# First loads beside the constants, time steps in eight matmuls, B by C in another bank, and running sums spread for half of the heads and both tiles at a time

## The chip, the cores and the metric

One core of one Trainium2 chip runs the whole program. The metric is the device time of one execution in microseconds; lower is better. Shown are the median of three runs and one profiled execution.

## The reference

Three layers act on 4096 tokens of 512 values, with a residual connection each: a feed-forward layer with a half weight, a Mamba-2 layer, and the same feed-forward layer again. Cut to what matters here:

```
# feed-forward: layer norm, 64 experts of which each token takes 4, and two shared experts
out = sum over the token's 4 experts of weight * down(silu(gate(h)) * up(h)) + shared(h)
x = x + 0.5 * out
# Mamba-2, batch 2, 2048 tokens, 8 heads of 128, state 128
proj = rmsnorm(layernorm(x)) @ in_proj_w            # gate 1024, ssm 1024, dt 8, B 128, C 128
ssm = silu(causal_conv4(ssm)); dt = softplus(dt + dt_bias)
cum = cumsum(A * dt)                                # the running sums, per head
y = (exp(cum_i - cum_j) * (C_i . B_j), j <= i) @ (dt * x)  +  exp(cum_i) * C_i @ state
state = exp(cum_end) * state + B' @ (exp(cum_end - cum_j) * dt * x)
x = x + ((y + D * ssm) * silu(gate)) @ out_proj_w
```

## The kernel before

Three phases follow each other on every engine, without a barrier between them: `ffn` "a" (to about 740 us), `mamba` (740 to 1645 us) and `ffn` "b". Matmuls whose inputs need full precision are split in high and low parts (`three`, lines 1568 to 1571: high by high, high by low, low by high), in `fp32r`. Each engine has its own program, written out by hand; the engines meet only in semaphores, so that a step starts when its engine has done all that stands ahead of it and its waits are met. Names: PE is TensorE, DVE VectorE, ACT ScalarE, POOL GpSimd, SP the engine that issues loads and stores.

**Mamba.** 16 blocks of 256 tokens (two tiles of 128). A projection writes 256 columns into one of two halves of the bank pair `p_ab`; the jobs of a block form a ring, and `ab(n, job)` waits until ACT has copied out the job two places before (`ab_free`). Gates 2 and 3 go to `p_x` instead. On PE a block is (`block_`, from line 1705): ssm 0 and 1, `cumulate` (running sums), the second half of the block before's output projection, ssm 2, `b_by_c`, `spread(0)`, ssm 3 to 5, `spread(1)`, ssm 6 and 7, gates 0 to 7, `x_to_tokens(0)`, `turn` (turns the next block's rows), `x_to_tokens(1)`, `y_product(0)`, `state_product(0)`, `head` (projections of dt, C and B for the next block), `y_product(1)`, `state_product(1)`, `to_tokens`, `out_product(0)`.

**The decays.** `spread` brings a tile's running sums of 8 heads to all partitions, in the bank pair `p_cr`: eight matmuls of 128 columns that pick a head. ACT takes the exponential of it (`carried`, line 1467, into `cdec`), DVE subtracts each token's own sum (`differences`, line 1851, eight instructions), after which PE may write `p_cr` again; ACT takes the exponential of the differences (`within`, line 1471), POOL multiplies `cdec` with C (line 1357), and DVE `decay` with the masked B by C (`by_cb`, line 1856). `diff_ready`, `cdec_exp`, `decay_exp` count these.

**DVE in a block.** `convolve(m)` is three steps in a row on `m_xt` (line 1862), each with two SBUF inputs; `split` and `by_cb` too. The order is: convolve 0 and 1, `ends`, `cum_lo`, `add_out` (line 1912), convolve 2, `mask_cb` (line 1844), `differences(0)`, convolve 3 to 5, `differences(1)`, convolve 6 and 7, `norm_stats`, `by_cb` twice, `norm_apply` (line 1799, what `turn` waits for), `times_dt`, `turned`, `norm_rest`, `skip_part(0)`, `gated(0)` (line 1897), `add_state(0)` (line 1907), and so on.

**ACT in a block.** `ssm_job(m)` is two instructions (lines 1436 and 1438). After `ssm_job(2)` come the copy of B by C, `carried(0)`, ssm 3 and 4, `within(0)`, ssm 5, `carried(1)`, ssm 6 and 7, gate 0, `within(1)`, gate 1, the silu of the first half of x, gates 2 to 4, the silu of the second half, gates 5 to 7 (copies of line 1410).

**Start and hand-over.** `make_constants` is a block of its own: no load is issued before POOL has built all constants. Then SP loads the first 512 rows (`a_xr`), the first piece of shared weights (`a_hr`), the first 256 rows again (`a_xs`), the router and more pieces. The rows are normalized, turned in two halves through one bank `p_ts` (`turn_s`), and the gate and up projections begin. DVE and ACT split each piece of weights in high and low parts (lines 556 and 896). At the end of `mamba`, `ffn` "b" begins early: `early(step)` of each engine is called from the last block. At the start of `ffn` "b"'s program DVE waits for the last store of `m_x` before it sets `chosen_before` to zero.

Of the kernel before, what the change touches and what calls it, by code (L numbers as in the profile page):

```python
# [136 lines left out]
def make_constants(nc, c, s):  # L137

    built = c.built = s("constants_built")
    c.BUILT = 21  # L140
    with nc.Block() as block:
        @block.gpsimd
        def _(pool):
            g = nc.gpsimd
            g.memset(c.ones[:], 1.0).then_inc(built, 1)
            g.memset(c.ident[:], 0.0).then_inc(built, 1)
            g.memset(c.neg_half[:], -0.5).then_inc(built, 1)
            g.memset(c.keep[:], 1.0).then_inc(built, 1)
            g.memset(c.cut[:], 0.0).then_inc(built, 1)
            g.memset(c.fold[:], 0.0).then_inc(built, 1)  # L150
            g.memset(c.picks[:], 0.0).then_inc(built, 1)
            pool.wait_ge(built, 7)

            g.memset(c.keep[:, NM // 2:NM // 2 + 1], 0.0).then_inc(built, 1)
            g.memset(c.cut[:, NM // 2:NM // 2 + 1], -1e30).then_inc(built, 1)
            g.affine_select(out=c.ident[:], in_=c.ident[:], compare_op=ALU.not_equal, fill=1.0, base=0,
                            pattern=[[-1, P]], channel_multiplier=1).then_inc(built, 1)

            g.affine_select(out=c.upto[:], in_=c.ones[:], compare_op=ALU.is_ge, fill=0.0, base=0,
                            pattern=[[1, P]], channel_multiplier=-1).then_inc(built, 1)  # L160
            g.affine_select(out=c.before[:], in_=c.ones[:], compare_op=ALU.is_ge, fill=0.0, base=-1,
                            pattern=[[1, P]], channel_multiplier=-1).then_inc(built, 1)

            g.affine_select(out=c.fold[:], in_=c.fold[:], compare_op=ALU.not_equal, fill=1.0, base=0,
                            pattern=[[-1, E]], channel_multiplier=1).then_inc(built, 1)

            g.affine_select(out=c.picks[:], in_=c.picks[:], compare_op=ALU.not_equal, fill=1.0, base=0,
                            pattern=[[-1, NH]], channel_multiplier=1).then_inc(built, 1)
            pool.wait_ge(built, 14)
            g.affine_select(out=c.fold[:], in_=c.fold[:], compare_op=ALU.not_equal, fill=1.0, base=-E,  # L170
                            pattern=[[-1, E]], channel_multiplier=1).then_inc(built, 1)
            g.affine_select(out=c.picks[:], in_=c.picks[:], compare_op=ALU.not_equal, fill=1.0, base=-LO_AT,
                            pattern=[[-1, NH]], channel_multiplier=1).then_inc(built, 1)

            g.iota(c.token_no[:], pattern=[[P, TILES]], base=1, channel_multiplier=1,
                   allow_small_or_imprecise_dtypes=True).then_inc(built, 1)
            g.iota(c.slot_no[:], pattern=[[P, PAIRS]], base=0, channel_multiplier=1,
                   allow_small_or_imprecise_dtypes=True).then_inc(built, 1)
            g.iota(c.spare_row[:], pattern=[[0, 1]], base=T, channel_multiplier=1,
                   allow_small_or_imprecise_dtypes=True).then_inc(built, 1)  # L180
            g.tensor_copy(c.ones_bf[:], c.ones[:]).then_inc(built, 1)
            g.iota(c.expert_no[:], pattern=[[1, E]], base=0, channel_multiplier=0,
# [1942 lines left out]
```

## Time and profile before

| | us |
|---|---|
| median of 3 runs | 2400.81 (2399.59 to 2406.45) |
| the profiled execution | 2399.49 |
| its span | 2397.7 |
| PE busy | 2338.3 (98%) |
| DVE busy | 1413.8 (59%) |
| ACT busy | 955.8 (40%) |
| POOL busy | 665.3 (28%) |
| a block of mamba (1032.12 to 1088.70) | 56.58 |

The span runs from the first to the last instruction of the program on the chip. A matmul's duration in the rows is from its issue to its modelled end, so that matmuls in a stream overlap; how far apart they start is what each costs. Busy is an average over phases: what a wait is worth is read from the place where it stands.

### The profile page before, as it was taken

The numbers are of one execution on the slowest core, as the hardware profiler recorded it, in microseconds if no ns is written. First come the engines' busy times: TensorE is split into PE (matmuls) and PEld (weight loads), VectorE is DVE, ScalarE is ACT, GpSimd is POOL, SyncE is SP. The second block draws the span as 40 slices with busy tenths as digits, with TensorE's granted clock in tenths as the row PEclk, the third lists the DMA queues.
The fourth block names the chain that finished last, engine by engine and source line by source line (L and its number), as shares of the span: only waits on it lengthen the run. The fifth ranks groups of instructions, "written<-read, shape, count | busy, mean of one in ns | idle before, by whom it ended". The sixth has DMA issues, their size and how long they took to land.

```text
span 2397.7 us, 41942 instructions
## 1 busy us (share of the span) xinstructions
PE 2338.3 (98%) x16732; PEld 2061.0 (86%) x16732; DVE 1413.8 (59%) x3236; ACT 955.8 (40%) x1665; POOL 665.3 (28%) x524
## 2 busy tenths in 40 slices
PE   5999999999998999999999999998999999999998
PEld 5999999777798888888888888887999999877787
DVE  6777762223228777777777777777777764232221
ACT  4332322333336455544545555454333332233321
POOL 1244443121221322222222222221044444121221
PEclk9999999999999999999999999999999999999999
DMA  7644213899844111111111111103254320799958
GB/s 254 197 156 150 85 63 125 265 279 281 242 99 130 36 28 27 27 27 27 27 27 27 27 27 27 27 18 135 84 195 145 109 97 20 255 286 276 282 117 176
DMA packets 102754, 292.82 MB, mean 122 GB/s; under 512 B 22498, under 2 KB 22754, under 8 KB 91872
## 3 DMA queue, kind: packets, MB, share of 16 engines
q1 hardware_dynamic: 55216, 198.87, 23.2%
q0 software_dynamic: 47344, 91.27, 17.0%
q8 instruction: 134, 2.20, 0.4%
q14 instruction: 60, 0.49, 0.1%
HBM read 197.28 MB, written 151.80 MB: 146 GB/s over the span
## 4 chain that ended last, share of the span: by engine, by line
PE 95%; DVE 2%; issue 1%; ACT 1%; DMA 1%; DVEq 0%; SPq 0%; ACTq 0%
PE m_p_ab L1569 5%; PE m_p_ab L1571 5%; PE m_p_ab L1570 5%; PE m_p_x L1569 3%; PE m_p_x L1571 3%; PE m_p_x L1570 3%; PE p_up_a L697 3%; PE p_up_b L697 3%; PE p_gate_a L697 3%; PE p_up_a L699 3%; PE p_up_a L698 3%; PE m_p_y L1670 3%; PE p_gate_a L698 3%; PE p_gate_b L697 3%; PE p_gate_a L699 3%; PE p_x_b L797 3%
## 5 line engine op out<-in xcount | busy, mean ns | idle before, releaser
L1862 DVE SCALAR_TENSOR_TENSOR m_xt<-m_ssm,m_convw,m_xt 128x256 f32<-128x256 f32 x384 | 218.9, 583 | 57.5 <-ACT m_ssm L1438 48.4
L1569 PE MATMUL m_p_ab<-m_ht_hi,m_wi_b_hi 128*128 128x256 f32 x640 | 182.0, 284 | 3.9 <-ACT m_ssm L1438 2.3
L1571 PE MATMUL m_p_ab<-m_ht_hi,m_wi_b_lo 128*128 128x256 f32 x640 | 179.3, 280 | 0.0
L1570 PE MATMUL m_p_ab<-m_ht_lo,m_wi_b_hi 128*128 128x256 f32 x640 | 179.2, 280 | 0.0
L448 POOL DMA_INDIRECT slot_rows<-a_hr,a_slot_now x128 | 130.4, 1019 | 151.4 <-PE p_gate_a L699 96.2
L448 POOL DMA_INDIRECT slot_rows<-b_hr,b_slot_now x128 | 129.9, 1015 | 151.4 <-PE p_gate_b L699 96.1
L697 PE MATMUL p_gate_a<-a_hts_hi,a_w_hi 128*128 128x256 f32 x512 | 148.6, 290 | 1.7 <-DVE a_hts_lo L978 1.4
L697 PE MATMUL p_gate_b<-b_hts_hi,b_w_hi 128*128 128x256 f32 x512 | 148.4, 290 | 0.3
L697 PE MATMUL p_up_b<-b_hts_hi,b_w_hi 128*128 128x256 f32 x512 | 147.7, 289 | 0.0
L697 PE MATMUL p_up_a<-a_hts_hi,a_w_hi 128*128 128x256 f32 x512 | 147.7, 288 | 0.0
L699 PE MATMUL p_gate_a<-a_hts_hi,a_w_lo 128*128 128x256 f32 x512 | 145.4, 284 | 0.0
L698 PE MATMUL p_gate_a<-a_hts_lo,a_w_hi 128*128 128x256 f32 x512 | 145.4, 284 | 0.0
L698 PE MATMUL p_gate_b<-b_hts_lo,b_w_hi 128*128 128x256 f32 x512 | 145.2, 284 | 0.0
L699 PE MATMUL p_gate_b<-b_hts_hi,b_w_lo 128*128 128x256 f32 x512 | 145.2, 284 | 0.0
L699 PE MATMUL p_up_a<-a_hts_hi,a_w_lo 128*128 128x256 f32 x512 | 144.7, 283 | 0.0
L699 PE MATMUL p_up_b<-b_hts_hi,b_w_lo 128*128 128x256 f32 x512 | 144.6, 282 | 0.0
L698 PE MATMUL p_up_b<-b_hts_lo,b_w_hi 128*128 128x256 f32 x512 | 144.4, 282 | 0.0
L698 PE MATMUL p_up_a<-a_hts_lo,a_w_hi 128*128 128x256 f32 x512 | 144.4, 282 | 0.0
L984 DVE TENSOR_TENSOR b_prod<-b_silu,p_up_b 128x512 f32<-128x512 f32 x64 | 44.0, 688 | 165.9 <-PE p_up_b L699 134.6
L1344 POOL TENSOR_TENSOR m_state_dec<-m_state,m_etot 128x1024 f32<-128x1024 f32 x31 | 59.3, 1914 | 279.7 <-ACT m_etot L1454 244.4
L1569 PE MATMUL m_p_ab<-m_ht_hi,m_wi_a_hi 128*128 128x256 f32 (+1 forms) x448 | 134.2, 300 | 1.2 <-ACT m_ssm L1438 1.2
L984 DVE TENSOR_TENSOR a_prod<-a_silu,p_up_a 128x512 f32<-128x512 f32 x64 | 44.0, 687 | 150.3 <-PE p_up_a L699 133.4
(352 smaller groups left out, 7440.5 us busy)
## 6 DMA issues: line engine op xcount, KB each, us to landing
a_ew<-in_ew SPq DMA_DIRECT2D x32, 1536.0 KB, 7.5
b_ew<-in_ew SPq DMA_DIRECT2D x32, 1536.0 KB, 8.3
after_ffn<-a_zeros POOLq DMA_DIRECT2D x6, 2048.0 KB
out<-b_zeros POOLq DMA_DIRECT2D x6, 2048.0 KB
slot_rows<-a_zeros POOLq DMA_DIRECT2D x1, 8336.0 KB, 36.9
a_rows<-slot_rows SPq DMA_DIRECT2D x32, 260.5 KB, 8.3
b_rows<-slot_rows SPq DMA_DIRECT2D x32, 260.5 KB, 9.0
a_xr<-in_x SPq DMA_DIRECT2D x8, 1024.0 KB
```

The source lines that it names most:

```text
L448: g_.indirect_dma_start(out=xg, out_offset=bass.IndirectOffsetOnAxis(ap=slot_now[r % HR][:, at:at + 1], axis=0), in_=hr[r % HR][:, j, :], ...
L697: t.matmul(out, l_hi, r_hi_, start=first, stop=False)
L698: t.matmul(out, l_hi, r_lo_, start=False, stop=False)
L699: return t.matmul(out, l_lo, r_hi_, start=False, stop=last)
L797: mm = t.matmul(p_x1[e * CAP:(e + 1) * CAP, 0:2 * F], xt[:, q % 2, k, e * CAP:(e + 1) * CAP], w[q % EU][:, e, k * 2 * F:(k + 1) * 2 * F], ...
L984: v.tensor_tensor(prod[:, i % 2, :, :], silu[:, i % 2, :, :], p_up[:, :, :], ALU.mult).then_inc(prod_ready, 1)
L1344: g.tensor_tensor(state_dec[:], state[:], etot[:, j, :].unsqueeze(2).to_broadcast([P, NH, HP]), ALU.mult).then_inc(state_dec_ready, 1)
L1569: t.matmul(out, l_hi, r_hi_, start=first, stop=False)
L1570: t.matmul(out, l_hi, r_lo_, start=False, stop=False)
L1571: return t.matmul(out, l_lo, r_hi_, start=False, stop=last)
L1670: t.matmul(out, xdt[j][:, hd, :], decay[j][:, hd, :], start=True, stop=False)
L1862: ins_ = v.scalar_tensor_tensor(xt[:, m, :], ssm[:, m, i:i + BM], convw[:, m, i:i + 1], xt[:, m, :], ALU.mult, ALU.add)
```

## The change

Named by the functions:

- **Start.** `make_constants` runs ahead of POOL's program inside the main block, and the engines that need constants wait for `c.built`. The first rows are loaded in halves (`load_first_rows`), the first piece of weights between them. The first 256 rows are normalized from `xr`. `norm_stats(0)` and `inv_std(0)` work in halves, in both FFNs; in "a" `norm_apply(0)` comes after the second weight piece's split. The second half of the first turning goes to the bank of `p_gate` (`turned_in`), in both FFNs. `chosen_before` is set to zero in `choose_best(0)`, and with it moves DVE's wait for the last store.
- **Time steps.** The weights of dt stand in `w_dt` (high, zeros, low: 40 columns), so that two matmuls per 128 inputs give high and low part in rows of their own; `to_tokens` adds them with `picks` in a real matmul and no longer turns them.
- **B by C.** It is computed right after `cumulate`, into `p_y`; DVE masks it from there, ahead of `add_out`. ACT's copy and the job in the ring are gone; gate 4 goes to `p_y` too.
- **Running sums.** `spread(i)` takes four heads and both tiles, four matmuls of 256 columns. `carried(i)` is two exponentials, one per tile, of four heads each; `differences(i)` and `within(i)` the same four heads of both tiles. POOL waits for both `carried`, then multiplies both tiles.
- **State.** `add_state(0)` comes before `gated(0)`.

```diff
@@ mamba, POOL
                 decay_state(0)
+                pool.wait_ge(cdec_exp, n * 2 + 2)
                 for j in range(TM):
-                    pool.wait_ge(cdec_exp, n * TM + j + 1)
                     g.tensor_tensor(cdec[j][:], cdec[j][:],
                                     ct[:, j * P:(j + 1) * P].unsqueeze(1).to_broadcast([P, NH, P]),
                                     ALU.mult).then_inc(cdec_ready, 1)
@@ mamba, ACT
-                wait(act, decay_ready, n * TM)
-                copy_job(n, J_CB, cb[:, :, :])
-                def carried(j):
-                    wait_apart(c, a, (cr_full, n * TM + j + 1), (y_full, n * TM))
-                    bias = {"bias": c.cut[:, n:n + 1]} if j == 0 else {}
-                    a.activation(cdec[j][:], heads(p_cr), ACT.Exp, **bias).then_inc(cdec_exp, 1)
-                def within(j):
-                    act.wait_ge(diff_ready, (n * TM + j) * NH + NH)
-                    a.activation(decay[j][:], decay[j][:], ACT.Exp).then_inc(decay_exp, 1)
+                def carried(i):
+                    wait_apart(c, a, (cr_full, n * 2 + i + 1), (y_full, n * TM))
+                    for j in range(TM):
+                        bias = {"bias": c.cut[:, n:n + 1]} if j == 0 else {}
+                        ins_ = a.activation(cdec[j][:, i * HH:(i + 1) * HH, :], wide(p_cr)[:, :, j * P:(j + 1) * P],
+                                            ACT.Exp, **bias)
+                    ins_.then_inc(cdec_exp, 1)
+                def within(i):
+                    act.wait_ge(diff_ready, (n * 2 + i) * NH + NH)
+                    part = decay_both[:, :, i * HH:(i + 1) * HH, :]
+                    a.activation(part, part, ACT.Exp).then_inc(decay_exp, 1)
@@ mamba, PE: the ring, time steps, B by C, running sums
-                if job in J_GATE[2:4]:
+                if job in IN_X:
                     wait(pe, out_ready, n * TM)
+                elif job in IN_Y:
+                    wait(pe, y_read, n * TM)
                 else:
-                    before = job - 4 if job in J_GATE[4:6] else job - 2
-                    if n * JOBS + before >= 0:
-                        pe.wait_ge(ab_free, n * JOBS + before + 1)
+                    at = RING.index(job)
+                    before = n * JOBS + RING[at - 2] - (JOBS if at < 2 else 0)
+                    if before >= 0:
+                        pe.wait_ge(ab_free, before + 1)
...
+            def project_dt(n):
...
+                for k in range(KD):
+                    for part in (ht_hi, ht_lo):
+                        mm = t.matmul(out, w_dt[:, k, :], part[:, k, :], start=(k == 0 and part is ht_hi),
+                                      stop=(k == KD - 1 and part is ht_lo))
...
-                    mm = t.matmul(out[:, at:at + NH], dtt[:, j * P:(j + 1) * P], c.ident[0:NH, 0:NH],
-                                  is_transpose=True, start=True, stop=True)
+                    t.matmul(out[:, at:at + NH], dtt[:, j * P:(j + 1) * P], c.picks[0:CR, :], start=True, stop=True)
...
-                for hd in range(NH):
-                    mm = t.matmul(heads(p_cr)[:, hd, :], pick[:, hd:hd + 1].to_broadcast([CR, P]),
-                                  cum_rows[:, j * P:(j + 1) * P], start=True, stop=True)
+                for at in range(HH):
+                    hd = i * HH + at
+                    mm = t.matmul(wide(p_cr)[:, at, :], pick[:, hd:hd + 1].to_broadcast([CR, P]),
+                                  cum_rows[:, :], start=True, stop=True)
@@ mamba, DVE
             def by_cb(n, j):
-                dve.wait_ge(decay_exp, n * TM + j + 1)
+                dve.wait_ge(cb_ready, n + 1)
+                dve.wait_ge(decay_exp, n * 2 + 2)
...
                     if more:
+                        add_state(n, 0)
                         gated(n, 0)
-                        add_state(n, 0)
@@ ffn: SP, DVE of "a"; the turnings
-                    sp.dma_start(xr[:], src_r[0]).then_inc(xr_loaded, 16)
-                    for o in range(PIECES):
+                    load_first_rows(0)
+                    load_piece(0)
+                    load_first_rows(1)
+                    load_router()
+                    for o in range(1, PIECES):
                         load_piece(o)
-                        if o == 0:
+                        if o == 2:
                             load_xs(0)
-                            load_router()
...
-                    v.memset(chosen_before[:], 0.0)
-                    norm_stats(0)
+                    norm_first(0)
                     split(0)
-                    norm_apply(0)
                     turned_s(0, 0)
                     turned_s(0, 1)
-                    for o in range(1, 4):
-                        split(o)
-                else:
-                    dve.wait_ge(prior.x_stored[0], prior.LAST_STORED)
-                    v.memset(chosen_before[:], 0.0)
+                    split(1)
+                    norm_first(1)
+                    dve.wait_ge(c.built, c.BUILT)
+                    norm_apply(0)
+                    split(2)
+                    split(3)
...
+        turned_in = lambda b, half: p_gate if b == 0 and half == 1 else p_ts
```

How the change moves instructions, at two places. POOL in a block of mamba, from the decay of the state to the next norm, before:

```order
L1344 TENSOR_TENSOR m_state_dec<-m_state,m_etot 128x1024 [waits m_state_ready,m_etot_ready] x2
L1357 TENSOR_TENSOR m_cdec<-m_cdec,m_ct 128x1024 [waits m_cdec_exp] x2
L1327 DMA m_x_181<-after_ffn 128x2x512 [waits m_x_loaded0]
L1321 TENSOR_TENSOR m_inv_193<-m_var_192,neg_half 128x4 [waits m_var_ready]
L1351 TENSOR_TENSOR m_xs<-m_xdt,m_to_end 128x1024 [waits m_xdt_ready,m_ends_ready,m_s_full] x2
```

and now:

```order
L1392 TENSOR_TENSOR m_state_dec<-m_state,m_etot 128x1024 [waits m_state_ready,m_etot_ready] x2
L1405 TENSOR_TENSOR m_cdec<-m_cdec,m_ct 128x1024 [waits m_cdec_exp]
L1405 TENSOR_TENSOR m_cdec<-m_cdec,m_ct 128x1024
L1375 DMA m_x_133<-after_ffn 128x2x512 [waits m_x_loaded0]
L1369 TENSOR_TENSOR m_inv_145<-m_var_144,neg_half 128x4 [waits m_var_ready]
L1399 TENSOR_TENSOR m_xs<-m_xdt,m_to_end 128x1024 [waits m_xdt_ready,m_ends_ready,m_s_full] x2
```

The two multiplies of `m_cdec` each had a wait; now the first has one, for more, and the second none.

DVE in the same block, from the running sums' low part to the end of the first `differences`, before:

```order
L1839 TENSOR_TENSOR m_cum_rows<-m_cum_t,m_cum_rows 8x256 [waits m_cum_hi_ready]
L1912 TENSOR_TENSOR m_x_215<-m_p_x,m_x_215 128x512 [waits m_out_full]
L1862 SCALAR_TENSOR_TENSOR m_xt<-m_ssm,m_convw,m_xt 128x256 [waits m_ab_free]
L1862 SCALAR_TENSOR_TENSOR m_xt<-m_ssm,m_convw,m_xt 128x256 [waits m_dve_step] x2
L1844 TENSOR_TENSOR m_cb<-m_cb,upto 128x256 [waits m_ab_free]
L1851 TENSOR_SCALAR m_decay<-m_p_cr,m_cum 128x128 [waits m_y_full,m_cdec_exp,m_dve_step]
L1851 TENSOR_SCALAR m_decay<-m_p_cr,m_cum 128x128 x7
```

and now:

```order
L1908 TENSOR_TENSOR m_cum_rows<-m_cum_t,m_cum_rows 8x256 [waits m_cum_hi_ready]
L1913 TENSOR_TENSOR m_cb<-m_p_y,upto 128x256 [waits m_cb_full]
L1985 TENSOR_TENSOR m_x_167<-m_p_x,m_x_167 128x512 [waits m_out_full]
L1935 SCALAR_TENSOR_TENSOR m_xt<-m_ssm,m_convw,m_xt 128x256 [waits m_ab_free]
L1935 SCALAR_TENSOR_TENSOR m_xt<-m_ssm,m_convw,m_xt 128x256 [waits m_dve_step] x2
L1923 TENSOR_SCALAR m_decay<-m_p_cr,m_cum 128x128 [waits m_y_full,m_cdec_exp]
L1923 TENSOR_SCALAR m_decay<-m_p_cr,m_cum 128x128 x7
```

The mask of B by C has moved ahead of the addition to `m_x` (the output projection's second half), and `differences` follows the convolution directly.

## Rows read from the trace of the kernel before

**Rows 1.** The page: busy time by engine; the chain that ended last, by engine.

```profile
PE 2338.3 (98%) x16732; PEld 2061.0 (86%) x16732; DVE 1413.8 (59%) x3236; ACT 955.8 (40%) x1665; POOL 665.3 (28%) x524
PE 95%; DVE 2%; issue 1%; ACT 1%; DMA 1%; DVEq 0%; SPq 0%; ACTq 0%
```

**Rows 2.** Who waited for whom, TensorE: total us, times, longest us.

```profile
PE p_x_b L749 <- DVE b_htr_lo L922: 4.9, 1, 4.9
...
PE p_ts_b L707 <- DVE b_hts_lo L978: 4.1, 1, 4.1
...
PE m_p_y L1670 <- DVE m_state L1907: 3.4, 15, 0.3
```

**Rows 3.** Windows: stretch, us, busy (instructions) by engine, granted clock, DMA share, GB/s.

```profile
1648.90:1652.20 3.30, 3.07 (x15) 3.10 (x16) 1.40 (x3) 0.60 (x1) 0.00 (x0) 0.50 0.01 2
1676.20:1682.90 6.70, 5.93 (x26) 5.78 (x27) 4.02 (x5) 1.23 (x2) 0.00 (x0) 0.50 0.42 141
```

**Rows 4.** In order of time, TensorE, one block: start, us, instruction.

```profile
1047.76 0.28 PE L1569 MATMUL m_p_ab<-m_ht_hi,m_wi_a_hi 128*128 128x256 f32 x1
...
1049.17 0.61 PE L1630 MATMUL m_p_ab<-m_ct,m_bt 128*128 128x128 f32 x4
1049.71 1.10 PE L1642 MATMUL m_p_cr<-m_cum_rows,m_pick 40*128 40x128 f32 x8
...
1069.05 0.28 PE L1569 MATMUL m_p_ab<-m_ht_hi,m_wi_b_hi 128*128 128x256 f32 x1
...
1071.34 0.49 PE L1578 MATMUL m_p_cr<-ident,m_h 128*128 128x128 f32 x3
```

**Rows 5.** The same view: turning the time steps, and the cumulate's small matmuls.

```profile
1032.43 0.29 PE L1611 MATMUL m_p_ab<-ident,m_dtt 8*128 8x8 f32 x2
...
1041.18 0.29 PE L1620 MATMUL m_p_ab<-m_la,upto 128*128 128x16 f32 x2
...
1041.62 0.60 PE L1623 MATMUL m_p_ab<-upto,m_la 128*8 128x128 f32 x4
```

**Rows 6.** The same view of the same block: POOL, the second tile's multiply.

```profile
1057.48 2.44 POOL L1357 TENSOR_TENSOR m_cdec<-m_cdec,m_ct 128x1024 f32<-128x1024 f32 x1 [2.98 <-ACT m_cdec L1467]
```

**Rows 7.** The same view of the same block: DVE.

```profile
1050.25 1.53 DVE L1862 SCALAR_TENSOR_TENSOR m_xt<-m_ssm,m_convw,m_xt 128x256 f32<-128x256 f32 x3 [1.60 <-ACT m_ssm L1438]
...
1052.15 2.16 DVE L1851 TENSOR_SCALAR m_decay<-m_p_cr,m_cum 128x128 f32<-128x128 f32 x8
1054.23 6.50 DVE L1862 SCALAR_TENSOR_TENSOR m_xt<-m_ssm,m_convw,m_xt 128x256 f32<-128x256 f32 x9
```

**Rows 8.** The same view of block 0: one DVE step, and POOL beside it.

```profile
773.67 7.21 DVE L1862 SCALAR_TENSOR_TENSOR m_xt<-m_ssm,m_convw,m_xt 128x256 f32<-128x256 f32 x1
...
773.51 2.36 POOL L1344 TENSOR_TENSOR m_state_dec<-m_state,m_etot 128x1024 f32<-128x1024 f32 x1
775.37 5.22 POOL L1357 TENSOR_TENSOR m_cdec<-m_cdec,m_ct 128x1024 f32<-128x1024 f32 x2
```

**Rows 9.** The same view of the block at 1050: ACT.

```profile
1054.61 1.06 ACT L1471 ACTIVATE m_decay<-m_decay 128x1024 f32<-128x1024 f32 x1
...
1062.83 1.06 ACT L1471 ACTIVATE m_decay<-m_decay 128x1024 f32<-128x1024 f32 x1 [1.62 <-DVE m_decay L1851]
...
1068.18 0.39 ACT L1410 ACTIVATE m_gate<-m_p_ab 128x256 f32<-128x256 f32 x1
```

**Rows 10.** The same view of the start.

```profile
4.47 0.44 SPq L400 DMA_DIRECT2D a_xr<-in_x  x1
...
22.28 0.58 PE L697 MATMUL p_gate_a<-a_hts_hi,a_w_hi 128*128 128x256 f32 x1 [1.41 <-DVE a_hts_lo L978]
...
39.32 0.63 PE L749 MATMUL p_x_a<-ident,a_hr 128*128 128x128 f32 x4 [2.84 <-DVE a_htr_lo L922]
```

**Rows 11.** The same view of the hand-over: DVE.

```profile
1644.96 1.21 DVE L1907 TENSOR_TENSOR m_state<-m_state_dec,m_p_cr 128x1024 f32<-128x1024 f32 x1
...
1675.23 0.09 DVE L1061 MEMSET b_chosen_before<- 128x32 uint32 x1 [2.87 <-DMA after_mamba<-m_x]
```

More of the change, by code:

```diff
@@ L134, in __exit__ @@
             self.nc.all_engine_barrier()
[L137 to L182, printed above, removed]
-                   allow_small_or_imprecise_dtypes=True).then_inc(built, 1)
-            pool.wait_ge(built, c.BUILT)
@@ L410, in program @@
                         sp.wait_ge(hr_ready, (b + 1) * TR)
+                        if b == 0 and not prior:
+                            sp.wait_ge(hs_mid, TS)
                         sp.dma_start(xr[:], src_r[b + 1]).then_inc(xr_loaded, 16)
@@ L702, in turn_s @@
                 pe.wait_ge(hs_ready, (b + 1) * TS)
-                wait(pe, hts_ready, 2 * b + half)
+                if b > 0:
+                    pe.wait_ge(hts_ready, 2 * b + half)
                 for kk in range(2):
@@ L993, in finish @@
                 dve.wait_ge(down_done, (b + 1) * UN)
+                if b == 0 and not prior:
+                    dve.wait_ge(xs_loaded[0], 16)
                 if b == NS - 1:
@@ L1144, in mamba @@
     CLEARED = len([name for name in prior.sems if name not in OWN])
-    JOBS = 6 + 2 * CI
-    J_DT, J_C, J_B, J_TOK, J_CUM, J_CB = 0, 1, 2, 3, 6, 8
-    J_SSM = [4, 5, 7, 9, 10, 11, 12, 13]
-    J_GATE = list(range(14, 22))
+    JOBS = 5 + 2 * CI
+    J_DT, J_C, J_B, J_TOK, J_CUM = 0, 1, 2, 3, 6
+    J_SSM = [4, 5, 7, 8, 9, 10, 11, 12]
+    J_GATE = list(range(13, 21))
+    IN_X, IN_Y = [J_GATE[2], J_GATE[3]], [None, J_GATE[4]]
+    RING = [job for job in range(JOBS) if job not in IN_X + IN_Y]
     with ExitStack() as ctx:
@@ L1213, in wi @@
         def wi(first, n):
+            if first == DT0:
+                return w_dt[:, :, 0:NH], w_dt[:, :, LO_AT:CR]
             if first < SPLIT_COL:
-                return [part[:, :, first:first + n] for part in wi_a]
+                return [part[:, :, first - NH:first - NH + n] for part in wi_a]
             i, at = divmod(first - SPLIT_COL, 2 * P)
@@ L1221, in mamba, with ab_of @@
         p_x, p_y, p_cr, p_ab = (ps(name, [P, 2, 512]) for name in ("p_x", "p_y", "p_cr", "p_ab"))
-        ab_of = lambda job: p_x[:, job % 2, :] if job in J_GATE[2:4] else p_ab[:, job % 2, :]
+        def ab_of(job):
+            for bank, jobs in ((p_x, IN_X), (p_y, IN_Y)):
+                if job in jobs:
+                    return bank[:, jobs.index(job), :]
+            return p_ab[:, RING.index(job) % 2, :]
         heads = lambda t: t[:, :, :].rearrange("p b (h q) -> p (b h) q", q=P)
+        wide = lambda t: t[:, :, :].rearrange("p b (h q) -> p (b h) q", q=BM)
+        HH = NH // 2
         flat = lambda t: t[:, :, :].rearrange("p a b -> p (a b)")
@@ L1710, in block_ @@
                 cumulate(n)
+                b_by_c(n)
                 if not is_(n, 0):
```

175 lines of the change are left out of this document (125 added, 50 removed).

## Prediction

> **What bounds the kernel now.** I read the page first. TensorE is busy 98% of the span, and the chain that ended last runs through it for 95% [rows 1]: time is gained by taking TensorE work away or by ending its waits, and lost by any new wait. The view of who waited for whom, for TensorE, comes next [rows 2]: one wait of 4.9 and one of 4.1 us at the hand-over to the second FFN, and 15 waits for `m_state` of 0.2 us each. The first projection of all starts at 22.28 us [rows 10]. In the middle of the mamba stage TensorE hardly waits at all, so there I looked for what is only just in time. The windows of granted clock show what a wait can cost besides itself [rows 3]: the clock stood at 0.50 in 1648.9 to 1652.2, right at the end of the 4.1 us wait, and in 1676.2 to 1682.9, at the end of the 4.9 us wait. At 0.50 (1.2 GHz) TensorE does half its work, so 3.4 us cost 1.7 us. The view in order of time of one middle block (period 56.6 us, 15 like it) then gives every term. I count from A, the start of the third ssm projection at 1047.76 [rows 4].
>
> **TensorE work, per block.** The running sums: eight matmuls of 128 columns start 0.119 us apart (1.10 us less the 0.27 us of the last, over 7) [rows 4]; the projections of 256 columns are as close, 12 in the 1.41 us from 1047.76 to the row behind them (0.117 each). Eight of 256 columns in place of sixteen of 128 save 8 x 0.119 = 0.95 us. By the Trainium skill (TensorE: Matmul & The Clock Gate, Back-to-back issue gap) matmuls of 128 columns follow at about 81 ns and of 512 at 131; between them 256 would take about 98, and the saving be 16 x 81 - 8 x 98 = 0.51 us. The rows show one distance for both sizes, so I keep 0.95. The time steps: 12 matmuls become 8, at the same distance: 4 x 0.117 = -0.47. Turning the time steps becomes a real product with `picks` of twice the instructions: two go now in 0.22 us, as half of the four that start at 1041.18 and end before 1041.62 (0.44) [rows 5]: +0.22 (from 0 to 0.3). `add_state` ahead of `gated`: the wait of 0.22 goes, and no other is near. Sum: -1.42 us, and 15 blocks make -21.
>
> **What the waits on both halves do.** Each exponential of the carried part now covers half of the heads of both tiles, so neither multiply of `m_cdec` on POOL can start before the second half. Today each follows the exponential of its own tile: the first falls beside `differences`, the second starts at 1057.48 [rows 6] and lies beside the convolution, and nine steps that should take some 4.5 us (three alone take 1.53) take 6.50 [rows 7]: DVE loses 2 us to POOL. Block 0 shows the case of multiplies without a break: one convolution step is held for 7.21 us, until the last of three is done [rows 8].
>
> Now the new block. The convolution step group at A+2.49 stays [rows 7]; the mask is done earlier, in DVE's idle time before A, so `differences` starts at A+3.93 in place of A+4.39 and ends at A+6.09. ACT: from the start of `within(0)` to the multiply's start are 2.87 us [rows 6, 9], two half exponentials cost some 0.05 more, so POOL starts at A+9.04 and multiplies for 4.8 us, to A+13.84: the lone multiply takes 2.44 [rows 6], and the two of block 0 took 4.72 from the end of `m_state_dec` (775.87) to their own (780.59) [rows 8]. DVE, after six clean steps, begins the convolution of the sixth ssm job at A+8.97; its second step finds POOL in the way, is held to A+14.12 (0.28 behind POOL's end, as 780.88 is behind 780.59), and the third ends at A+14.64. The second `differences` takes 2.16 [rows 7] and ends at A+16.70, where today it ends at A+15.04. ACT's exponential `within(1)` follows at once, and from there to the end of the sixth gate copy ACT is busy for 5.74 us (1062.83 to 1068.57) [rows 9]: A+22.5. The last gate projection needs the buffer that this copy frees. Today it starts at A+21.29 [rows 4], 0.48 us after it could. TensorE would now want it at A+19.8 (1.5 earlier): B by C (0.54, 1049.17 to 1049.71 [rows 4]) lies ahead of A, the spreads are 0.95 shorter. **It waits 1.66 + 1.50 - 0.48 = 2.7 us.** `turn` (A+23.58 today) then starts at A+24.8; DVE's normed rows for it come some 7.9 us after `differences`, at A+24.6, just in time. Per block -1.42 + 2.68 = +1.3 us; 15 blocks +19. Block 0 gets nothing: its multiplies already run together, held back by the load of x.
>
> The Trainium skill (SBUF — State Buffer, Who interferes with whom) says that VectorE with two SBUF inputs and GpSimd share a port pair, which whoever is first has for its whole instruction. Taken by that, the held step would slip in between the two multiplies and the next one wait for the second; `differences` would end near A+17.0 and the 15 blocks cost 24 us, not 19. The 7.21 us row speaks for a hold over the whole run, and I go by the row.
>
> **Clock in the new waits.** Whether 2.7 us of waiting let the clock fall the trace doesn't say: the wait of 2.84 us before 39.32 [rows 10] did not, the wait of 4.12 did for 3.4 us, worth 1.7 us of work. Bounds are no fall and one in each of 15 blocks, 0 and 25 us; 2.7 lies nearer to 2.84, but fifteen times in a row is more often than once, so I take 7 falls, +12.
>
> **The start.** The constants move beside the loads: the first load is issued at about 0.8 us in place of 4.47 [rows 10], the first half of the rows does not wait for the second, the second turning has a bank of its own. The first projection could start 6 us earlier, at 16 in place of 22.28 [rows 10]: 3.7 from the issue, the rest from the half load and the second bank. But the wait that ends at 39.32 is one for DVE's `a_htr_lo` [rows 10], and DVE now does the statistics of the second half and `norm_apply` behind the first turnings, ahead of the pieces of weights that this wait needs; its work up to there is the same and only its first wait is shorter. So the ends are -6 (all of the earlier start kept) and +1 (the longer queue of DVE alone), and since the row names DVE I take -2.
>
> **The hand-over.** `turn_s(0, 1)` gets its own bank: the wait of 4.1, from 1645.0, becomes one of 1.2 for `m_state`, which ends at 1646.17 [rows 11], and the 3.3 us of half clock behind it [rows 3] go: -2.9 - 1.7 = -4.6. The wait of 4.9 ended late because DVE stood until 1675.23 for a store [rows 11]; that wait is now behind `choose_best`. DVE's work behind it can then start 2.9 us earlier, so the wait is 2.0: -2.9; of the 3.4 us that 6.7 us at half clock cost I take 2.1, since a shorter fall is possible: -5.0. Sum -9.6 (from -4, the two waits halved with the clock as it is, to -10.5).
>
> **Sum.** -2 - 9.6 + 19 + 12 = +19.4, some 20, on the profiled execution's 2399.5 us (span 2397.7); the median of the runs is 1.3 higher. I forecast 2420 us. A change of 0.3%, 7 us, is about what a measurement can tell from none.
>
> **Rivals.** (1) Faster: POOL does not hold DVE longer than today, because the multiplies fall beside `differences` (decisive: POOL has to start after the second step, later than A+9.5, where I have A+9.04). Then `differences` ends at A+14.6, the last gate waits 0.6, a block gives 0.8 back to all 1.4, and with start and hand-over the time is 2400 - 12 - 12 to 2400 - 12 - 21, 2367 to 2376. For it: half a microsecond decides, and ACT's halves are not in the trace. Against it: POOL starts from the same exponential that today reaches it within DVE's seventh step. Chance 0.20. (2) No change: the hold is as forecast and the clock never falls, or hand-over and start give more: 2394 to 2408, chance 0.14. (3) The wide matmuls cost by columns, so that nothing is saved in the spreads: TensorE then waits 1.7 in place of 2.7 us and the time is the same, since DVE sets it; it counts only under rival 1, where 14 us of the gain go. (4) The clock falls in every block and DVE's first step is held too (+0.5 us a block): 2400 + 8 + 25 + 8, 2441; in the forecast's own chance.
>
> **Numbers.** Forecast (slower) 0.66, no change 0.14, faster 0.20. Range 2378 to 2441: it leaves out most of rival 1 and the far end; the forecast's own is 2405 to 2441.
>
> **What would show it.** Right: TensorE's list of waits has a new line, projections in `m_p_ab` waiting for ACT's `m_gate`, near 15 times 2.7 us; one DVE step `m_xt` of 4.5 to 5 us in each block; the two `m_cdec` multiplies without a gap; spread rows x4, 0.6 us; no wait for `m_state`; the period of a block near 58 us; more stretches at 0.50; the waits of 4.9 and 4.1 shrunk. Wrong: a block period under 56 us, or convolution steps of 0.5 us beside the multiplies.

## The result, and the profile after

The changed kernel takes 2422.14 us (median of 4 runs, 2418.91 to 2425.29), the kernel before 2400.2 us beside it (2399.42 to 2406.45): a ratio of 1.0086, 95% interval 1.0063 to 1.0108. It is slower by 22 us. The forecast was 2420. Rows, waits and stages below are those of one profiled execution of each kernel.

The page and the view of who waited for whom (total us, times, longest us), the changed kernel. They answer to [rows 1] and [rows 2]:

```profile
span 2421.8 us, 41670 instructions
PE 2327.8 (96%) x16572; PEld 2055.6 (85%) x16572; DVE 1422.3 (59%) x3240; ACT 950.5 (39%) x1682; POOL 685.0 (28%) x526
PE 83%; DVE 9%; ACT 4%; issue 2%; DMA 1%; DVEq 0%; POOL 0%; SPq 0%; ACTq 0%
```

```profile
PE m_p_ab L1619 <- ACT m_gate L1458: 42.6, 16, 3.3
...
PE p_gate_b L713 <- DVE b_hts_lo L1009: 2.6, 1, 2.6
...
PE p_x_b L766 <- DVE b_htr_lo L951: 2.0, 1, 2.0
...
PE m_p_y L1739 <- DVE m_state L1980: 1.0, 1, 1.0
```

TensorE is 10 us less busy and still later. Its share of the chain that ended last fell from 95 to 83%, and DVE and ACT have 13% between them in place of 3. The first wait is new in blocks 1 to 15, where it is 2.62 us each time (42.6 less the 3.3 of block 0, over 15; block 0 had 1.5 before). The 15 waits for `m_state` are gone but for the one at the hand-over; the wait of 4.9 us is 2.0, the one of 4.1 us is 1.0.

One block in order of time: TensorE, DVE, POOL and ACT (start, us, instruction, the idle time before it and its releaser). A, the start of the third ssm projection, is 1051.75 here.

```profile
1051.75 0.28 PE L1619 MATMUL m_p_ab<-m_ht_hi,m_wi_a_hi 128*128 128x256 f32 x1
...
1053.26 0.72 PE L1710 MATMUL m_p_cr<-m_cum_rows,m_pick 40*128 40x256 f32 x4
...
1071.19 0.28 PE L1621 MATMUL m_p_ab<-m_ht_hi,m_wi_b_lo 128*128 128x256 f32 x1
1074.09 0.58 PE L1619 MATMUL m_p_ab<-m_ht_hi,m_wi_b_hi 128*128 128x256 f32 x1 [2.63 <-ACT m_gate L1458]
```

```profile
1055.69 2.15 DVE L1923 TENSOR_SCALAR m_decay<-m_p_cr,m_cum 128x128 f32<-128x128 f32 x8
1057.76 8.44 DVE L1935 SCALAR_TENSOR_TENSOR m_xt<-m_ssm,m_convw,m_xt 128x256 f32<-128x256 f32 x9
...
1061.14 2.51 DVE L1935 SCALAR_TENSOR_TENSOR m_xt<-m_ssm,m_convw,m_xt 128x256 f32<-128x256 f32 x1
...
1063.69 2.51 DVE L1935 SCALAR_TENSOR_TENSOR m_xt<-m_ssm,m_convw,m_xt 128x256 f32<-128x256 f32 x1
1066.12 2.15 DVE L1923 TENSOR_SCALAR m_decay<-m_p_cr,m_cum 128x128 f32<-128x128 f32 x8
```

```profile
1060.81 5.11 POOL L1405 TENSOR_TENSOR m_cdec<-m_cdec,m_ct 128x1024 f32<-128x1024 f32 x2 [10.49 <-ACT m_cdec L1512]
```

```profile
1068.30 1.06 ACT L1519 ACTIVATE m_decay<-m_decay 128x1024 f32<-128x1024 f32 x1 [4.51 <-DVE m_decay L1923]
1069.27 0.36 ACT L1458 ACTIVATE m_gate<-m_p_ab 128x256 f32<-128x256 f32 x1
1069.65 1.28 ACT L1524 ACT_TABLE_LOAD   x1
1070.94 1.06 ACT L1524 ACTIVATE m_xt<-m_xt 128x1024 f32<-128x1024 f32 x1
1071.91 0.64 ACT L1458 ACTIVATE m_gate<-m_p_x 128x256 f32<-128x256 f32 x2
1072.43 0.39 ACT L1458 ACTIVATE m_gate<-m_p_y 128x256 f32<-128x256 f32 x1
1072.70 1.06 ACT L1524 ACTIVATE m_xt<-m_xt 128x1024 f32<-128x1024 f32 x1
1073.64 0.67 ACT L1458 ACTIVATE m_gate<-m_p_ab 128x256 f32<-128x256 f32 x2
```

Read it from the top. POOL's two multiplies run as one stretch of 5.11 us. The nine convolution steps beside them take 8.44 us, where they took 6.50 [rows 7]; the two rows of one step each, cut out of the nine, show where: each sits beside one multiply and ends 0.28 us after it. So the second `differences` starts at A+14.37 and ends at A+16.5; ACT, idle for 4.51 us, takes its exponential at A+16.55, and behind it a gate copy, a table load, half a silu, three copies and the other half, all ahead of the sixth gate copy, whose end lets TensorE go on at A+22.34. TensorE wanted to at A+19.7.

The granted clock (columns as in [rows 3]): behind that wait TensorE runs at 1.2 GHz.

```profile
1073.40:1080.20 6.80, 6.11 (x28) 6.11 (x29) 4.25 (x9) 3.79 (x6) 1.50 (x1) 0.50 0.00 0
1698.10:1701.50 3.40, 3.40 (x19) 3.40 (x18) 2.67 (x3) 0.14 (x1) 0.00 (x0) 0.50 0.45 120
```

Of the 15 waits 11 are followed by a stretch at 0.50, nine of 3.4 us and two of 6.8. Blocks without one last 57.4 us (57.41, from the held step at 1003.73 to the one at 1061.14), those with 3.4 us at 0.50 some 58.8, those with 6.8 us 60.0. The row of 1698.10 is the hand-over, where 3.4 us at 0.50 are left of 3.3 and 6.7 [rows 3].

Where the time went, by stage, each figure rounded by itself. The mamba stage is counted from TensorE's first matmul with a name in `m_` to the first of the second FFN.

| us | before | after | difference |
|---|---|---|---|
| to the first matmul of mamba | 739.0 | 735.7 | -3.3 |
| mamba | 905.4 | 936.2 | +30.8 |
| second FFN, to the end of the span | 753.3 | 750.0 | -3.3 |
| span | 2397.7 | 2421.8 | +24.1 |

### The profile page after: what moved, and what is told of

It is laid out like the page before. It is cut to its first block, busy times and chain, and to the rows that moved or that the text cites. A ratio compares the mean times of both kernels' runs of the same rounds, so it can differ in the third digit from the quotient of the medians.

```text
span 2421.8 us, 41670 instructions
## 1 busy us (share of the span) xinstructions
PE 2327.8 (96%) x16572; PEld 2055.6 (85%) x16572; DVE 1422.3 (59%) x3240; ACT 950.5 (39%) x1682; POOL 685.0 (28%) x526
## 4 chain that ended last, share of the span: by engine, by line
PE 83%; DVE 9%; ACT 4%; issue 2%; DMA 1%; DVEq 0%; POOL 0%; SPq 0%; ACTq 0%
DVE m_xt L1935 5%; DVE m_decay L1923 3%; PE p_up_b L713 3%; PE p_up_a L713 3%; PE p_gate_b L713 3%; PE p_gate_b L715 3%; PE p_gate_b L714 3%; PE p_up_b L715 3%; PE p_up_b L714 3%; PE p_up_a L715 2%; PE p_up_a L714 2%; PE p_gate_a L713 2%; PE p_x_a L814 2%; PE p_x_b L814 2%; PE p_gate_a L714 2%; PE p_gate_a L715 2%
## 5 line engine op out<-in xcount | busy, mean ns | idle before, releaser
L1935 DVE SCALAR_TENSOR_TENSOR m_xt<-m_ssm,m_convw,m_xt 128x256 f32<-128x256 f32 x384 | 248.0, 659 | 58.1 <-ACT m_ssm L1486 48.8
L1619 PE MATMUL m_p_ab<-m_ht_hi,m_wi_b_hi 128*128 128x256 f32 x576 | 168.4, 292 | 45.2 <-ACT m_gate L1458 42.6
L1621 PE MATMUL m_p_ab<-m_ht_hi,m_wi_b_lo 128*128 128x256 f32 x576 | 164.4, 285 | 0.0
L1620 PE MATMUL m_p_ab<-m_ht_lo,m_wi_b_hi 128*128 128x256 f32 x576 | 164.4, 285 | 0.0
L1619 PEld LDWEIGHTS m_p_ab<-m_ht_hi,m_wi_b_hi 128*128 128x128 f32 x576 | 112.7, 196 | 50.8 <-ACT m_gate L1458 42.3
L1392 POOL TENSOR_TENSOR m_state_dec<-m_state,m_etot 128x1024 f32<-128x1024 f32 x31 | 74.0, 2389 | 255.3 <-ACT m_etot L1502 255.3
```

Source lines behind the costliest of these rows:

```text
L1392: g.tensor_tensor(state_dec[:], state[:], etot[:, j, :].unsqueeze(2).to_broadcast([P, NH, HP]), ALU.mult).then_inc(state_dec_ready, 1)
L1619: t.matmul(out, l_hi, r_hi_, start=first, stop=False)
L1620: t.matmul(out, l_hi, r_lo_, start=False, stop=False)
L1621: return t.matmul(out, l_lo, r_hi_, start=False, stop=last)
L1935: ins_ = v.scalar_tensor_tensor(xt[:, m, :], ssm[:, m, i:i + BM], convw[:, m, i:i + 1], xt[:, m, :], ALU.mult, ALU.add)
```

## The experiments

Eight kernels ran. The table gives each kernel's median, its stages as above, and, for blocks 1 to 15, TensorE's wait and the clock behind it, both from its profiled execution; the ratios are to the kernel before, run beside it (medians 2401.3 and 2401.2 in the two sets of runs).

| | median us | ratio (95%) | mamba | second FFN | `m_gate` wait per block | blocks with the clock at 0.50 behind it |
|---|---|---|---|---|---|---|
| before | 2400.2 | | 905.4 | 753.3 | none | 0 |
| the change | 2422.1 | 1.0086 (1.0063 to 1.0108) | 936.2 | 750.0 | 2.62 | 11 |
| halves on POOL | 2382.0 | 0.9902 (0.9872 to 0.9932) | 891.0 | 754.9 | 0.78 | 0 |
| start and hand-over alone | 2386.7 | 0.9938 (0.9917 to 0.9959) | 905.5 | 742.6 | none | 0 |
| spread by tile | 2373.7 | 0.9880 (0.9854 to 0.9905) | 893.7 | 743.1 | none | 0 |
| gate copies first | 2404.3 | 1.0005 (0.9985 to 1.0025) | 915.6 | 756.1 | 1.4 | 0 |
| multiplies beside differences | 2367.3 | 0.9846 (0.9826 to 0.9865) | 877.5 | 752.6 | none | 0 |
| the same, gate copies first | 2367.7 | 0.9854 (0.9841 to 0.9867) | 879.0 | 752.8 | none | 0 |
| waits between multiplies | 2427.2 (one run) | | 933.3 | 756.9 | 2.6 | 10 |
| second gate copy first | 2409.1 | 1.0023 (1.0008 to 1.0038) | 928.6 | 751.3 | 2.36 | 9 |

My theory was that POOL's two whole multiplies hold two convolution steps, and that this, through ACT's queue, makes the gate projection wait. The rival was that ACT's own order makes its copy late, whatever POOL does.

**1. The multiplies by halves of heads.**

```diff
-pool.wait_ge(cdec_exp, n * 2 + 2)
-for j in range(TM):
-    g.tensor_tensor(cdec[j][:], cdec[j][:], ct_j, ALU.mult).then_inc(cdec_ready, 1)
+for i in range(2):
+    pool.wait_ge(cdec_exp, n * 2 + i + 1)
+    for j in range(TM):
+        part = cdec[j][:, i * HH:(i + 1) * HH, :]
+        ins_ = g.tensor_tensor(part, part, ct_j, ALU.mult)
+        if i:
+            ins_.then_inc(cdec_ready, 1)
```

(`ct_j` stands for C of tile j, broadcast over the heads.)

> The change, but POOL multiplies m_cdec in four pieces of half the heads: two right after the first carried exponentials, two after the second. Theory (POOL's two whole multiplies hold two convolution steps for 2.5 us each, and this delays the second differences, the ACT chain and the last gate projection): the first pair falls beside the first differences, the second pair holds steps for about 2.5 us in all, not 5; TensorE's wait of 2.62 us for m_gate falls to 0 to 0.4 us, and most of the 11 falls of the clock in it go. 2422 - 15 x 2.4 - 11 to 22 = 2364 to 2375 us. Rival (ACT's own chain sets the gate buffer, its exponentials of halves being late, whatever POOL does): the wait stays over 2 us and the time over 2410 us.

One block, POOL and DVE, and TensorE's waits:

```profile
1043.56 2.83 POOL L1407 TENSOR_TENSOR m_cdec<-m_cdec,m_ct 128x512 f32<-128x512 f32 x2 [5.04 <-ACT m_cdec L1515]
1049.02 2.73 POOL L1407 TENSOR_TENSOR m_cdec<-m_cdec,m_ct 128x512 f32<-128x512 f32 x2 [2.63 <-ACT m_cdec L1515]
```

```profile
1045.97 6.58 DVE L1938 SCALAR_TENSOR_TENSOR m_xt<-m_ssm,m_convw,m_xt 128x256 f32<-128x256 f32 x9
```

```profile
PE m_p_ab L1622 <- ACT m_gate L1461: 15.4, 16, 3.7
...
PE p_gate_b L713 <- DVE b_hts_lo L1009: 4.1, 1, 4.1
```

The same work on POOL in another cut takes 1.86 us off the nine steps (8.44 to 6.58), and the wait falls by 1.84 (2.62 to 0.78). The rival falls as it stands, "whatever POOL does"; what ACT's order adds is the matter of experiment 4. The clock does not fall behind a wait of 0.78 us, and the mamba stage is 45 us shorter than in the change. I had expected the wait at 0.4 at most and 2375 us at most, and both are missed: the nine steps are no faster than before (6.50), while TensorE wants the buffer earlier; and the second FFN is 12 us longer than in experiments 2 and 3, with waits of 2.0 and 4.1 us that they don't have and the clock at 0.50 behind both (below).

**2. Start and hand-over alone**: the kernel before with the change's FFN functions and its constants beside the loads.

> The kernel before with the change's first rows, constants beside the loads, and FFN waits only; the mamba stage is the one before. Theory: start -2 to -4, hand-over -9.6, so 2386 to 2389 us; the wait of 4.9 us near 2.0, the wait for m_state after the hand-over near 1.2. Rival (the hand-over's gain is taken by what comes later): 2396 to 2400 us.

2386.7 us, 14.6 under the kernel before beside it (2401.3) and inside what I expected. To the first matmul of mamba 735.3, so -3.7; mamba 905.5, unchanged; second FFN -10.7. TensorE's waits there are the forecast's: 0.99 for `m_state`, 1.97 for `b_htr_lo`, and the clock does not fall there at all.

**3. The spreads by tile**, everything else as in the change.

```diff
-for at in range(HH):
-    hd = i * HH + at
-    t.matmul(wide(p_cr)[:, at, :], pick_hd, cum_rows[:, :], ...)
+for hd in range(NH):
+    t.matmul(heads(p_cr)[:, hd, :], pick_hd, cum_rows[:, i * P:(i + 1) * P], ...)
```

(`pick_hd` stands for the column of `pick` that picks the head. `carried`, `differences`, `within` and POOL's wait go back to one tile at a time with it.)

> The change with its running sums spread per tile as before (sixteen matmuls of 128 columns, each multiply behind its own tile's exponential); first rows, time steps and B by C as in the change. Theory: one held step of 2.5 us per block as before, no wait for m_gate; per block -0.47 +0.22 -0.22 = -0.5 us, so 2400 - 13 - 7 = 2380 us (2376 to 2385). Rival (B by C and the gate projection's new banks bring the wait, not the wide spreads): a wait for m_gate of over 1 us stays, 2400 us or more.

2373.7 us, faster than expected, and no wait for `m_gate` but one in block 0. In each of the 15 blocks one convolution step is held for 2.51 us, as in the kernel before; in the change it is two. So time steps, B by C and the gate's new banks bring no wait. The mamba stage is 11.7 us shorter than before, 0.78 a block where I had 0.47: the wait for `m_state` was worth more than its 0.22 us (TensorE's two starts there, 0.50 us apart before, are 0.12 apart now). Between this and the change stand 42.4 us of mamba, all of it the price of spreading wide with whole multiplies: the wide spreads by themselves save TensorE work, as experiment 5 shows.

**4. ACT's order: the second gate copy ahead of `within(1)`, the sixth ahead of `silu_half(1)`.**

```diff
 gate_job(0)
-within(1)
 gate_job(1)
+within(1)
 silu_half(0)
-for m in range(2, 5):
+for m in range(2, 6):
     gate_job(m)
 silu_half(1)
-for m in range(5, CI):
+for m in range(6, CI):
     gate_job(m)
```

> The change with ACT's second gate copy ahead of the second within exponential, and its sixth gate copy ahead of the second silu; POOL as in the change. Theory (the chain behind the second differences is ACT: exponential, gate copy, table load, silu, copies, silu, sixth gate copy): the copy comes 0.4 + 1.0 us earlier, the wait of 2.62 becomes 1.2 us, and the clock falls less often: 2422 - 15 x 1.4 - 5 to 20 = 2381 to 2396 us. Rival (the wait is set by another thing than this order): the wait and the time stay, 2415 us or more.

TensorE's waits, blocks 1 to 15:

```profile
PE m_p_ab L1619 <- ACT m_gate L1458: 21.3, 15, 1.4
PE m_p_cr L1628 <- DVE m_h L1868: 12.0, 14, 0.9
```

The granted clock from 830 to 1600 us, with 14 of the waits for `m_gate` in it (columns as in [rows 3]):

```profile
830.00:1600.00 770.00, 738.19 (x5332) 662.49 (x5332) 588.83 (x1230) 387.21 (x710) 229.66 (x110) 1.00 0.11 27
```

The wait falls to 1.4 us, as worked out, so this chain on ACT is the one; and the clock falls in none of blocks 1 to 15. But 2404.3 us is 8 above my range: a wait that I had not seen takes its place. `turn` now waits 0.9 us for the rows that DVE norms behind the same held steps. I had taken ACT's order to be the only path from the hold to TensorE; a second one, through DVE, lies less than 1 us behind. And the second FFN is slow in this kernel too. Its ten executions lie 19 us apart, from 2396.2 to 2414.8 us.

**5. Each pair of half multiplies beside the differences of its half.**

```diff
 pool.wait_ge(cdec_exp, n * 2 + i + 1)
+pool.wait_ge(diff_ready, (n * 2 + i) * NH + 1)
```

> The first experiment's four half multiplies, each pair now waiting for the first step of its own half's differences. Theory (what delays the gate copy is the convolution steps held by POOL, 1.53 and 1.40 us in place of 0.49 in the first experiment; differences, which read PSUM, are not held): differences stay at 0.34 us a step, at most one or two convolution steps of up to 1.3 us remain, the second differences end some 1.5 to 2 us earlier, the wait of 0.78 us for m_gate goes, the period of a block falls from 55.6 to 54.8 us; mamba stage 891 - 12 = 879 us, whole 2362 to 2370 us. Rival 1 (differences are held too): the period stays at 55.6. Rival 2 (the turning of the normed rows becomes the wait, since the multiplies now hold the last convolution steps): a wait of 0.3 to 1 us for m_h, 2370 to 2380 us.

```profile
1041.59 2.55 POOL L1408 TENSOR_TENSOR m_cdec<-m_cdec,m_ct 128x512 f32<-128x512 f32 x2 [5.86 <-DVE m_decay L1927]
1048.74 2.54 POOL L1408 TENSOR_TENSOR m_cdec<-m_cdec,m_ct 128x512 f32<-128x512 f32 x2 [4.60 <-DVE m_decay L1927]
```

```profile
1041.10 2.15 DVE L1927 TENSOR_SCALAR m_decay<-m_p_cr,m_cum 128x128 f32<-128x128 f32 x8
1043.17 5.17 DVE L1939 SCALAR_TENSOR_TENSOR m_xt<-m_ssm,m_convw,m_xt 128x256 f32<-128x256 f32 x9
1048.25 2.15 DVE L1927 TENSOR_SCALAR m_decay<-m_p_cr,m_cum 128x128 f32<-128x128 f32 x8
1050.33 3.73 DVE L1939 SCALAR_TENSOR_TENSOR m_xt<-m_ssm,m_convw,m_xt 128x256 f32<-128x256 f32 x6
```

The multiplies lie beside `differences`, which takes 2.15 us as ever; only what sticks out behind it holds one convolution step. The nine steps take 5.17 us, the wait for `m_gate` is gone, a block lasts 54.6 us (from 1000 to 1054.6 TensorE is busy for 54.55), and mamba is 28 us shorter than before. Against experiment 3, with its narrow spreads, that is 1.2 us a block less. Both rivals fall. The Trainium skill (SBUF — State Buffer, Who interferes with whom) says that a DVE instruction with at most one SBUF input and no two-port mode does not contend with GpSimd. These rows agree: `differences` reads a PSUM tile and is 2.15 us with and without POOL beside it, the convolution reads two SBUF tensors and is held. At 2367.3 us this kernel is, with the next one, the fastest of the study, 1.5% under the one before.

**6. The same with ACT's order of the fourth experiment.**

> The kernel of the other run with multiplies beside the differences, and ACT's second and sixth gate copies ahead as in the experiment on that order. Theory (the m_gate wait is already gone without it): no change against that run, 2362 to 2370 us. Rival (a wait for m_gate is still there and this order ends it): up to 0.8 us a block less, 12 us below that run.

2367.7 us, no difference from experiment 5. ACT's order has nothing to give once the hold is gone.

**7. Waits between POOL's operations**, in the change.

```diff
 for j in range(TM):
+    pool.wait_ge(cdec_ready if j else state_dec_ready, n * TM + 1)
     g.tensor_tensor(cdec[j][:], ...)
```

> The change, with a wait on POOL's own semaphore ahead of each multiply of m_cdec, so that none starts before the one ahead has ended. Theory (the hold over a whole run of POOL operations, 7.50 us in block 0, needs operations that overlap by 0.5 us, as they do there alone): in block 0 the held steps become two or three of about 2.5 us; in the other blocks, where the multiplies overlap by 0.04 us and hold two steps of 2.5 us, nothing changes; 2418 to 2426 us. Rival (block 0's hold has another cause, its descriptors or the operands): the 7.5 us step stays.

Block 0, POOL and DVE, first in the change, then in this kernel:

```profile
770.33 2.36 POOL L1392 TENSOR_TENSOR m_state_dec<-m_state,m_etot 128x1024 f32<-128x1024 f32 x1
772.19 5.22 POOL L1405 TENSOR_TENSOR m_cdec<-m_cdec,m_ct 128x1024 f32<-128x1024 f32 x2
...
770.20 9.98 DVE L1935 SCALAR_TENSOR_TENSOR m_xt<-m_ssm,m_convw,m_xt 128x256 f32<-128x256 f32 x6
```

```profile
769.15 2.36 POOL L1392 TENSOR_TENSOR m_state_dec<-m_state,m_etot 128x1024 f32<-128x1024 f32 x1
771.66 4.95 POOL L1406 TENSOR_TENSOR m_cdec<-m_cdec,m_ct 128x1024 f32<-128x1024 f32 x2
...
769.18 2.62 DVE L1936 SCALAR_TENSOR_TENSOR m_xt<-m_ssm,m_convw,m_xt 128x256 f32<-128x256 f32 x1
...
769.18 5.17 DVE L1936 SCALAR_TENSOR_TENSOR m_xt<-m_ssm,m_convw,m_xt 128x256 f32<-128x256 f32 x2
```

In the change six steps take 9.98 us, 7.50 of them in the first alone. With the waits one step takes 2.62 us and two take 5.17; the third is like the second (2.51 each). So the run of POOL operations holds one step as a whole where each starts 0.5 us before the one ahead has ended (in block 0 the second starts at 772.19 and the first ends at 772.69), and with the overlap gone DVE is held for one operation at a time. The 0.04 us by which the multiplies overlap in the other blocks don't bring the long hold. Why POOL's operations overlap by 0.5 us in block 0 alone no run shows. In the other blocks nothing changes: two steps of 2.5 us, the wait 2.6. The time, 2427.2 us in its one execution, is 1 us above the range that I expected.

**8. The second gate copy alone ahead of `within(1)`.**

> The change with only the second gate copy moved ahead of the second within exponential. It takes 0.36 us off the chain on ACT: the wait of 2.62 us becomes 2.26. Theory 1 (whether the clock falls depends on the length of the wait, somewhere between 1.4 us, where it did in none of 15 blocks, and 2.6, where it did in 11): fewer falls than 11, and so a gain of 5 us from the waits and 1.7 us for each window of 3.4 us at 0.50 that goes, 2400 to 2417 us. Theory 2 (2.3 us is as bad as 2.6): 11 falls, 2415 to 2419 us.

The wait is 2.36 us (33.0 over 14, below), the clock falls in 9 blocks, mamba is 7.5 us shorter than in the change: 15 x 0.26 = 3.9 us of waits, and the rest from fewer and shorter stretches at 0.50 (nine of 3.4 us, none of 6.8).

```profile
PE m_p_ab L1619 <- ACT m_gate L1458: 33.0, 14, 2.4
```

Set beside experiments 1 and 4 this gives what the trace of before could not: behind 15 waits of 0.78 and 15 of 1.4 us the clock never fell, behind 2.36 it fell 9 times, behind 2.6 10 and 11 times. The counts, 9 against 11, are too near to say by themselves that 2.36 is better than 2.62. The time speaks for theory 1: the median of seven executions, 2409.1 us, lies within its 2400 to 2417 and below the 2415 to 2419 of theory 2, and the profiled one, where the nine were counted, is the longest of the seven, at 2417.1 with a granted clock of 0.987 against 0.988 to 0.991 in the others.

The length of the wait is not all, though. At the hand-over TensorE waits 1.97 us for `b_htr_lo` in every changed kernel. Behind it the clock fell in the change and in experiments 1, 4 and 7, and stayed up in experiments 2, 3, 5, 6 and 8; the wait of 2.62 us near the end of the change's second FFN was not followed by a fall either. What decides between them the runs don't show.

**The second FFN.** It takes 743 us in experiments 2 and 3 and 750 to 757 in the other kernels that ran. In these others ACT waits for a scatter before it can write the rows of an expert, and the rows of the next gate projection stand behind it on ACT. The changed kernel, ACT:

```profile
2331.66 0.60 ACT L636 ACTIVATE b_y<-p_x_b 128x512 f32<-128x512 f32 x1 [6.25 <-DMA out<-b_y,b_row_no]
2332.16 0.59 ACT L590 ACTIVATE b_hts_hi<-p_ts_b 128x512 fp32r<-128x512 f32 x1
```

TensorE pays with 2.6 us in the change and 4.5 in experiment 5. The scatters land one behind another, in the end 5.6 to 5.8 us apart, in experiments 2 and 3 as well. ACT has waits of 2.2 to 8.1 us for them in the seven kernels with the longer stage and none above 1.0 in experiments 2 and 3; that they are what makes it longer is argued from this, not tested. What pushes them just too late in some kernels I did not find: experiment 5 ran between 2357.1 and 2370.4 us.

## Why the prediction was right

The time, the sign and the mechanism held: POOL's two multiplies hold DVE, and through ACT's queue the last gate projection waits 2.6 us in every block. Point by point, forecast against the trace:

| | forecast | measured |
|---|---|---|
| second `differences` ends | A+16.70 | A+16.5 |
| last gate projection wanted | A+19.8 | A+19.7 |
| last gate projection starts | A+22.5 | A+22.34 |
| wait for `m_gate`, 15 blocks | 2.7 | 2.62 |
| TensorE's work per block | -1.42 | -1.8 (57.41 - 2.62 - 56.58) |
| clock falls | 7, +12 us | 11, +17.7 us |
| mamba | +31 | +30.8 |
| start | -2 (-6 to +1) | -3.3 |
| first projection | 16 | 15.48 |
| hand-over | -9.6 | -10.7 alone, -3.3 in the change |

The clock's +17.7 is nine blocks of 58.8 and two of 60.0 less 11 of 57.41. Three terms were off. Two of them, the work and the clock, cancel to within 1 us: that mamba came out at +30.8 for +31 is luck.

**The work saved was larger than -1.42**, by 0.4 us a block or 6 us. The spreads were priced too high: from the first start of a spread to what follows, 1.03 us before and 0.66 now, so 0.75 us for two and not 0.95. The 0.119 us was a mean over seven distances, of which the first is 0.16 and the others 0.11. In the wide spreads (the four matmuls of 1053.26, 0.72 us where I said 0.6) the distances are 0.22, 0.117 and 0.113. So twice the columns cost hardly more, and the first distance, which is paid once in either form, got longer. By the Trainium skill (TensorE: Matmul & The Clock Gate, Back-to-back issue gap) it would have been 0.51, an estimate from that section's figures; the measured 0.75 lies midway. More came from the wait for `m_state`: time steps and wait together gave 0.90 us and not 0.69. Turning cost 0.20, as forecast. Another 0.2 us lies in the projections: those of 256 columns into `p_x` start 0.113 us apart in all seven kernels with wide spreads and 0.118 apart in the kernel before and in experiments 2 and 3, at a granted clock of 1.00 in both; in experiment 5 that is worth 0.5 us a block against experiment 3. Why, no run shows. Some 0.1 us I can't place.

**The clock fell 11 times, not 7**, and twice for twice as long: 6 us more. The bounds of 0 and 25 held it. I had set one wait of 2.84 us without a fall against fifteen of 2.7; in the change 11 of 15 such waits brought one, and in experiment 7 it was 10.

**The hand-over** is right for the waits (1.0 and 2.0, forecast 1.2 and 2.0), and alone it gives 10.7. In the change 7.4 us of this are lost again. I find 8.0: 1.4 in the 3.4 us at 0.50 that are left, 2.6 in the wait near the end of the second FFN, and 4.0 behind TensorE's last matmul, where the span goes on for 14.4 us and in experiment 2 for 10.4. The forecast had no term for the last two.

**The start** went as argued. The first projection starts 6.8 us earlier (22.28 to 15.48), but TensorE then waits 6.7 us for `a_htr_lo` in place of 4.3, and its clock is at 0.50 from 25.5 to 32.4; 3.3 us are left. With this 1.3 us better than forecast, the spans of the profiled executions come out 24.1 us apart, against +19.4; the medians are 21.9 apart.

**The step that failed, though its result held, is "its second step finds POOL in the way, is held to A+14.12".** No single step is held over both multiplies, and the one step of 4.5 to 5 us that I named as a sign did not come; two steps are held for 2.51 us each. The rule of the Trainium skill (SBUF — State Buffer, Who interferes with whom), which I had set aside for the 7.21 us of block 0 [rows 8], describes these two; the end that I worked out by it, A+17.0, was further off than mine. I got the end within 0.2 us because POOL's stretch sets it either way. Experiment 7 tells why the row misled: POOL's operations overlap by 0.5 us in block 0 and by 0.04 in the others. The row was read rightly and carried over to a place with another pattern.

Rival 1 (POOL does not hold DVE longer than before) is excluded by the 8.44 us row; POOL started at A+9.06, forecast A+9.04, decisive A+9.5. What it would have been worth experiment 5 shows, where the multiplies do lie beside `differences`: 2367 us, the lower end of the 2367 to 2376 that I gave. Rival 3, where the wide matmuls cost by columns and nothing is saved, falls: 0.75 of the 0.95 us came.

## What to carry to other kernels

When a change makes one engine's operation wait for more, look at what lies beside it at its new time: here one of two GpSimd multiplies, 2.5 us in each block, moved from beside steps that read PSUM to where the other one lay, beside steps that read two SBUF tensors, and 42 us went with it. This is where the first one was in the kernel before, beside the `differences` of 1052.15 [rows 7]:

```profile
1052.10 2.41 POOL L1357 TENSOR_TENSOR m_cdec<-m_cdec,m_ct 128x1024 f32<-128x1024 f32 x1 [5.37 <-ACT m_cdec L1467]
```

Cutting the operation in halves, each tied to the point where its neighbour does no harm, gave 1.5% where the same change with whole operations lost 0.9%. And in the mamba blocks a wait of 2.4 to 2.6 us in a stream of matmuls cost 1.4 us beyond itself in most blocks, and now and then 2.6, where one of 1.4 us cost nothing beyond.
